# One hundred unread matrix products of eight shapes between the first layer 0 and pair groups 4 to 7

## The reference

```python
def _L0_cond_ref(x, embedding, W0, b0, W1, b1, W2, b2, weight, bias_k):   # L2 and L3 alike
    h = jax.nn.gelu(embedding @ W0 + b0, approximate=False)
    h = jax.nn.gelu(h @ W1 + b1, approximate=False)
    att = jax.nn.softmax((h @ W2 + b2) / T, axis=-1)
    agg_w = jnp.einsum('bk,koi->boi', att, weight[..., 0])
    agg_b = att @ bias_k
    return jnp.einsum('boi,bih->boh', agg_w, x) + agg_b[:, :, None]
def _L1_cond_ref(x, c, weight, c_weight, bias):
    out = lax.conv_general_dilated(x, weight, window_strides=(1,), padding=[(4, 4)],
                                   dimension_numbers=('NCH', 'OIH', 'NCH'), feature_group_count=4)
    return out + jnp.einsum('nd,od->no', c, c_weight)[:, :, None] + bias[None, :, None]
x = x + L0(x); x = x + L1(x); x = x + L2(x); x = x + L3(x)
```

## Time and profile before

| | |
|---|---|
| time, median of 2 runs | 486.37 us (485.83 and 486.91) |
| profiled execution, span from the first to the last instruction | 485.3 us |
| TensorE busy | 476.9 us, 98% of the span |
| weight loads busy | 460.8 us, 95% |
| VectorE, ScalarE, GpSimd busy | 321.1, 250.2, 149.1 us |
| share of TensorE in the chain that ended last | 98% |

### The profile page before, as it was taken

The page is one execution under the profiler, slowest core; times in us unless marked ns, Lnnn a source line. Parts: engine busy times, 40 slices in busy tenths (PEclk is TensorE's granted clock), DMA queues, the critical chain, the costliest instruction groups (busy, mean ns, idle before and its releaser), DMA issues.

```text
span 485.3 us, 17899 instructions
## 1 busy us (share of the span) xinstructions
PE 476.9 (98%) x8003; PEld 460.8 (95%) x8003; DVE 321.1 (66%) x407; ACT 250.2 (52%) x416; POOL 149.1 (31%) x151
## 2 busy tenths in 40 slices
PE   8999999999999999999999999999999999999995
PEld 7988999999999999999999999999999999999994
DVE  2648687766676877767677866767787676767423
ACT  3664445456544554655445455544554555445344
POOL 2935162332143312313332231423323141431010
PEclk9999999999999999999999999999999999999998
DMA  8696987666546467674646677554656756551124
GB/s 272 212 335 156 316 235 223 210 219 212 188 121 213 145 218 217 213 216 130 204 144 205 199 219 219 174 172 141 209 181 219 217 189 200 131 204 55 58 89 174
DMA packets 38956, 92.88 MB, mean 191 GB/s; under 512 B 4568, under 2 KB 25440, under 8 KB 34912
## 3 DMA queue, kind: packets, MB, share of 16 engines
q1 hardware_dynamic: 38880, 91.73, 61.0%
HBM read 53.95 MB, written 37.77 MB: 189 GB/s over the span
## 4 chain that ended last, share of the span: by engine, by line
PE 98%; DMA 1%; issue 0%; DVEq 0%; DVE 0%
PE cv_ps L495 57%; PE aux_ps L476 19%; PE aux_ps L518 16%; PE cv_ps L434 2%; PE cv_ps L421 1%; PE aux_ps L421 1%; PE cv_ps L518 1%; DMA m_rep<-in_net_dram 1%; PE aux_ps L456 0%; PE cv_ps L400 0%; PE aux_ps L375 0%; PE cv_ps L375 0%; DVEq L68 0%; PE aux_ps L390 0%; PE aux_ps L445 0%
## 5 line engine op out<-in xcount | busy, mean ns | idle before, releaser
L495 PE MATMUL cv_ps<-x_hi,conv_lo 32*128 32x512 f32 x1536 | 324.9, 391 | 0.0
L495 PE MATMUL cv_ps<-x_hi,conv_hi 32*128 32x512 f32 x1536 | 324.4, 389 | 0.0
L495 PE MATMUL cv_ps<-x_lo,conv_hi 32*128 32x512 f32 x1536 | 324.2, 391 | 0.2 <-issue 0.2
L495 PEld LDWEIGHTS cv_ps<-x_lo,conv_hi 32*128 32x128 f32 x1536 | 228.0, 184 | 2.4
L495 PEld LDWEIGHTS cv_ps<-x_hi,conv_lo 32*128 32x128 f32 x1536 | 227.6, 183 | 2.5
L495 PEld LDWEIGHTS cv_ps<-x_hi,conv_hi 32*128 32x128 f32 x1536 | 226.6, 183 | 3.0 <-DVE x_lo L754 0.6
L763 DVE SCALAR_TENSOR_TENSOR x_lo<-cv_ps,d_all,x_hi 128x512 fp32r<-128x512 f32 x128 | 87.3, 745 | 130.0 <-ACT x_hi L609 129.9
L619 ACT ACTIVATE y_all<-aux_ps,e_all 128x512 f32<-128x512 f32 x124 | 75.2, 690 | 135.0 <-PE aux_ps L518 135.0
L476 PE MATMUL aux_ps<-x_hi,a_hi 32*128 32x512 f32 x512 | 116.5, 391 | 0.6 <-issue 0.6
L476 PE MATMUL aux_ps<-x_hi,a_lo 32*128 32x512 f32 x512 | 115.8, 388 | 0.0
L476 PE MATMUL aux_ps<-x_lo,a_hi 32*128 32x512 f32 x512 | 115.8, 388 | 0.0
(11 more groups left out here) (103 smaller groups left out, 519.0 us busy)
## 6 DMA issues: line engine op xcount, KB each, us to landing
x_sb<-in_x_dram SPq DMA_DIRECT2D x31, 1024.0 KB, 6.7
out_dram<-y_all SPq DMA_DIRECT2D x62, 512.0 KB, 7.6
a_rep<-a_pairs SPq DMA_DIRECT2D x64, 128.0 KB, 7.5
m_rep<-m_pairs SPq DMA_DIRECT2D x64, 128.0 KB, 6.8
a_pairs<-a_all SPq DMA_DIRECT2D x1, 1920.0 KB, 11.7
m_pairs<-m_all SPq DMA_DIRECT2D x1, 1792.0 KB, 13.4
m_all<-in_mix_dram SPq DMA_DIRECT2D x2, 512.0 KB, 5.7
x_sb<-in_x_dram SPq DMA_DIRECT2D x2, 512.0 KB, 7.6
```

What stands on the lines that cost most here:

```text
L495: mm = pe.matmul(cv_ps[:, g, :], w[rows(g), j, :], a[n % 2][rows(g), q, s:s + T], start=(i == 0), stop=(i == steps - 1))
```

## The change

A new function `shapes` is called once, between step 4 and step 5 above. It issues 100 products whose results are never read: each starts a new sum (`start=True`) in a bank of `prep_ps`, over which `quad_product(4)` to `quad_product(7)` then write. Weights are slices of `conv_hi`, data are slices of `conv_lo`. Nothing is removed and nothing else is moved.

| | products | rows each | row groups | data columns | weight columns |
|---|---|---|---|---|---|
| a | 4 | 128 | whole array | 512 | 128 |
| b | 8 | 64 | both halves in turn | 512 | 128 |
| c | 4 | 32 | the first only | 512 | 128 |
| d | 16 | 32 | four in turn | 512 | 128 |
| e | 16 | 32 | four in turn | 256 | 128 |
| f | 16 | 32 | four in turn | 512 | 32 |
| g | 16 | 32 | four in turn | 512, from column 1 on | 128 |
| h | 4 | 32 | four in turn | 128, 256, 384, 512 | 128 |
| i | 16 | 32 | four in turn | 512 | 128 |

```diff
+            def unread(group, height, wide, at=0, columns=P, weights=conv_hi, moving=conv_lo):
+                part = slice(height * group, height * (group + 1))
+                pe.matmul(prep_ps[group][0:columns, 0:wide], weights[part, group, 0:columns],
+                          moving[:].rearrange("p j m -> p (j m)")[part, at:at + wide], start=True, stop=True)
+
+            def shapes():
+                pe.wait_ge(conv_split, 2)
+                pe.wait_ge(m_out, RING)
+                for _ in range(4):
+                    unread(0, P, T)
+                for _ in range(4):
+                    for group in range(HALVES):
+                        unread(group, P // HALVES, T)
+                for _ in range(4):
+                    unread(0, CG, T)
+                for wide in (T, T // 2):
+                    for _ in range(4):
+                        for group in range(G):
+                            unread(group, CG, wide)
+                for _ in range(4):
+                    for group in range(G):
+                        unread(group, CG, T, columns=CG)
+                for _ in range(4):
+                    for group in range(G):
+                        unread(group, CG, T, at=1)
+                for group in range(G):
+                    unread(group, CG, P * (group + 1))
+                for _ in range(4):
+                    for group in range(G):
+                        unread(group, CG, T)
...
             in_turn([layer0_steps(0, p) for p in range(PH)])
+            shapes()
             for m in range(4, B // QUAD):
```

## The result

| | before | after |
|---|---|---|
| time, median of 2 runs | 486.37 us | 494.63 us (493.87 and 495.40) |
| ratio to before, 95% interval | | 1.0167 (1.0145 to 1.0189) |
| profiled execution: its time, its span | span 485.3 us | 495.40 us, span 493.6 us |
| TensorE busy | 476.9 us | 485.1 us |
| granted clock, mean | 0.996 | 0.999 |

The kernel is 8.3 us slower, 1.7%, within the 2% of the forecast.

The account below looks back on a forecast made before the run. TensorE was taken to bound the kernel, streaming without a hole from 30 us to the end. Streams 7.2 us plus changes of shape 1.2 us gave 8.4 us, from 486.4 to 494.8 us; range 493.3 to 497.0.

Parts of the forecast that it names:

- Bound: TensorE streams rounds without a hole from 30 us to the end; work put ahead of the lanes adds its full length.
- 0.23 us a round: New products lying side by side in the array, 512 data columns: 0.23 us a round; 29 such rounds are 6.70 us.
- The reading that the fill ran at the lower clock: Shape a: the fill's 0.238 us on 256 columns was at 1.2 GHz, so 512 columns at 2.4 GHz take 0.23.
- Rival 1: Shapes a, b, c: weight loads not hidden on the same rows, 1.3 us more, 496.1 us; chance 0.08.
- The change adds five such places [...] 1.2 us: Changes a to b, b to c, e to f, f to g, i to `quad_product(4)`: 0.3 us the last, 0.2 to 0.25 the others.
- The 0.29 us: Layer 0's last round to the first full product: 0.52 us instead of 0.23, so 0.29 lost from row groups to whole array.
- The new wait: `shapes` waits for `conv_split` 2 and `m_out` 4 ahead of a; charged 0 us.
- the cover of 0.7 us: ScalarE's fourth evacuation ended at 29.09, a could start at 29.83 earliest; a load later by more would put the excess on the path.
- What moves behind: Products 4 to 7 and lanes shift 8.4 us; SP sends the remaining products 0.35 us later; nothing new waits, nothing is absorbed.
- Rivals 2: Dear changes of shape: 0.64 us each, five cost 3.2 us, 496.8 us; over 2% from 0.5 us a change; chance 0.08.
- 3 (halves or 32 columns one after another): Products not side by side: b's halves +0.9 us, 495.7 (chance 0.06); f's four products +2.8 us, 497.6 (chance 0.03).
- Rival 4: Cheaper: changes between row tilings free, up to 0.2 us absorbed by later waits; 7.5 us more, 493.9 us; chance 0.10.

Follow-up runs that it names:

- the doubled kernel: The 100 new products issued twice, 200 in all, by a second call of `shapes` in the changed kernel; 500.97 us against 486.44 before, ratio 1.0290.
- the runs of 64 products: Two runs with 64 products on 512 columns in place of the 100, of 128 rows (500.03 us) or 64 rows (501.36 us), against 486.39 before.
- the run with the waits alone: Changed kernel with all 100 products left out and the two waits of `shapes` kept; 486.71 us against 486.44 before, ratio 1.0002.
- 64 rows: 64 products of 64 rows on 512 columns, all in the first half of the array, in place of the 100; 501.36 us against 486.39 before.
- blocks of 8: 32 products of 32 rows on 512 columns, eight in each row group one group after another, in place of the 100; 492.86 us against 486.39 before.
- blocks of 16: 64 products of 32 rows on 512 columns, 16 in each row group one group after another, in place of the 100; 507.33 us against 485.71 before.

## Why the prediction was right, point by point

**Bound.** Right. TensorE's chain took the whole length of the new products, the doubled kernel doubled it, and the lanes behind it kept their length.

**0.23 us a round for a, b, c, d, f, g, i.** Right: 0.231 for 32 rows (3.70 / 16) and 0.227 for 64 and 128 rows (the starts in the runs of 64 products), with 32 weight columns the same, and nothing extra for the start at column 1. The reading that the fill ran at the lower clock was needed for this, and the 14.75 us bear it out. Rival 1 (weight loads not hidden on the same rows) is out: 64 products in a row on the very same rows, with a load for each, come 0.227 us apart, and in the trace each load starts with the product before its own. By the Trainium skill (TensorE: Matmul & The Clock Gate, The mechanism) a load overlaps a running product only where the row group differs; the run contradicts this, and fits the exception that the same section makes for loads into a background weight buffer.

**e, 256 columns.** 0.52 us forecast. In the trace the first row group's four products start 0.115 us apart on average, 0.46 in all. Nearly right.

**h.** 0.23 forecast, about 0.1 measured, from the starts of the first row group: since groups run ahead, the ones with few columns go on at once, and the longest one began early. That was not in the forecast.

**Changes of shape: mis-sized.** The step "The change adds five such places [...] 1.2 us" failed in two ways. Two of the five, e to f and f to g, are none, since weight columns are no shape (3.70 us for 16 rounds in turn). The others cost 0.2 us, and the last, to `quad_product`, not 0.3 (3.77 against 3.57 us). Only three remain, 0.6 us in place of 1.2. The 0.29 us that I read between layer 0 and `quad_product` was counted from the first product of the last round. In the trace of the changed kernel the last product of that round starts 0.21 us after its first (29.56 and 29.35), and 29.88 is only 0.09 us late behind it; the other 0.1 us of a change is the late second product, which I had not counted there.

**The new wait.** Charged at 0, and 0 in the profile of the changed kernel and in the run with the waits alone. But the cover of 0.7 us was overrated: in two other executions (twice, 64 rows) TensorE did wait for ScalarE there, by 0.2 us.

**What moves behind.** Right. ScalarE's last four evacuations ended at 42.01 us, and SP sent the rest of the products at 42.69 instead of 42.65; the prediction had 0.35 us later. TensorE has no wait there.

**Sum.** The stretch was 7.65 us and not 8.4: 28 rounds of 0.23 are 6.4 us, e 0.46, h 0.1 and three changes 0.6, about 7.6. The predicted 494.8 us was still 0.2 us from the first median and 0.5 us from the second, because that error was partly made up by holes in the lanes of single executions, which no step of the prediction held. That the number came so near is luck; what it had right is the bound and the price of a round. Rivals 2 (0.5 us a change) and 3 (halves or 32 columns one after another) are out. Rival 4 had 7.5 us for the stretch, close to the 7.65 measured, for a partly wrong reason: it had the row tilings free, and they are not; the weight columns are.

## What to carry to other kernels

Where TensorE is the whole chain, inserted products cost their rounds. In fp32r with 512 columns one round was 0.23 us whatever the rows, so rows left idle are the whole loss. Group products by the number of rows, since each change of it cost 0.2 us, while a change between 128 and 32 weight columns cost nothing. The order among row groups needed care only beyond four products in one group. A long stretch in one row group of 32 cost twice: three quarters of the rows stood idle, and in the one execution that had such a stretch the granted clock fell to 0.50 as well.

## What the runs showed of the hardware that was not expected

- Row groups are not bound to the program's order: 16 products in blocks of four a group took 1.06 us, not 3.7. Each group held four products, the running one and three more (blocks of 8: 4.95 us, 20 rounds; blocks of 16: the second group began with the first one's 13th).
- 64 products in blocks of 16 in one row group at a time lowered the granted clock from 1.00 to 0.50 after almost 6 us while TensorE was shown busy all the time, and it stayed low for 17 us (one execution). With 64 or 128 rows busy it stayed at 1.00 for 14.8 us (one execution each).
- A change of the number of rows (128, 64, 32) cost 0.2 us, a change between 128 and 32 weight columns nothing.
- TensorE stops for 0.4 to 1.1 us at single places in the lanes, other ones in other executions, with no semaphore to wait for. All 15 of these holes (14 profiles) ended 1.2 to 1.8 us after a 16 KB transfer of the "instruction" queue had landed. They are a part of the scatter of this kernel's times; the landing of the last output is another.
